# A graph network kernel on one core: the sums over the edges of one destination tile moved from TensorE to GpSimd's adding indirect transfers

## Chip, cores and metric

The kernel runs on one core of a Trainium2 chip. The metric is the device time of one execution in microseconds, as a median of runs. The profile is one execution, recorded by the hardware profiler.

## The reference, cut to what matters

There are 3125 nodes with 128 features and 53125 edges, sorted by destination (25000 random edges in both directions, and one loop per node). `x` is normalised by row and rectified, and goes through a recurrent graph network of twelve steps; then its result, added to `x`, goes through two graph convolutions.

```python
h = tanh(relu(layernorm(x)) @ W_in + b_in)
deg = clip(segment_sum(ones, dst), 1)[:, None]
for _ in range(12):
    agg = segment_sum(h[src], dst) / deg              # sums over edges: the subject here
    diff = tanh(gelu(agg @ W1 + b1) @ W2 + b2)        # 128 -> 256 -> 128
    h = h + 0.5 * (diff - relu(clearance) * h)
x = x + h
x = x + gcn(relu(gcn(relu(layernorm(x)))))            # two more sums over edges
```

## The kernel before

**Layout.** The nodes are 25 tiles of 128 (the last of 53). The seven destination groups are six of 512 nodes (the sixth, tiles 21 to 24, has 437) and group 6, `TAIL`, which is tile 20 alone: 128 nodes. `state` [128, 25, 128] f32 holds the nodes' rows. The adjacency counts `adj` stay in SBUF in f16. A sum over edges is a product with `adj`: for each of 25 source tiles, `hi` and `lo` (the two f16 halves of the scaled state) are the stationary operands and the group's columns of `adj` move past. That is 49 matmuls for a group (the short tile has both halves in one), in `edge_sums`, line 715.

**Entry.** Edges are packed into one integer each and stored in DRAM; GpSimd fetches 128 consecutive ones per window of five destinations with five indirect transfers (line 524). In 52 batches VectorE writes one-hot matrices (line 1168, two instructions for a batch), TensorE multiplies them (line 611) and ScalarE writes the counts into `adj` (line 913). Beside the first 34 batches the entry rows are computed: GpSimd normalises tile after tile (line 530, 25 instructions), TensorE transposes and multiplies them (lines 587 to 605), ScalarE applies tanh. VectorE's loop has extra work at some batches: at batch 6 the degree norms and a flag (lines 1188 to 1191), at batch 8 the first `lo` (line 1151). If the flag says that an edge was missed, a general path runs; with the reference's inputs it doesn't.

**A step** (`step`, TensorE) has this order, written out by hand: the rest of group 0's sums, group 1's sums, then for g = 2 to 6: sums of g, `outputs(g-2)` (line 757, second product, four tiles by two halves), `hidden(g-1)` (line 748, first product); after group 6, `hidden(6)`, the first eight source tiles of the next step's group 0 (`HEAD`), `outputs(5)` and `outputs(6)`. `hid` and `act_out` have one buffer for the groups 0 to 5.

The other engines follow in fixed orders too. VectorE: for g = 0 to 5, `add_bias(g-2)` (line 1295), `update(g-2)` (line 1300), `means(g)` (line 1288, sums times inverse degree); then `means(6)` and the `lo` of the next step (line 1151) between the last biases and updates. ScalarE:

```python
for g in range(1, TAIL):
    if g >= 2:
        tanh(t, g - 2)        # line 955; waits for add_bias(g - 2)
    gelu(t, g - 1)            # line 946, two instructions; waits for hidden(g - 1) and for outputs(g - 2)
act.wait_ge(s_agg, (t + 1) * NG)   # all sums of the step done: hi may be overwritten
for g in range(4):
    next_hi(t, g)             # line 857
```

`outputs(g)` waits for both instructions of `gelu(g)`. Step 1 (`first_step`) has an order of its own; step 12 (`last_step` on VectorE) also adds `x`, computes the second normalisation (lines 1363 to 1394) and the first layer's `lo` between its biases and updates. In the steps GpSimd and the DMA queues have nothing to do.

## Time and profile before

| | us |
|---|---|
| median of 3 runs | 1300.9 (1300.74 to 1300.9) |
| the profiled execution: its own time / its span | 1300.27 / 1298.5 |
| TensorE (matmul) busy | 1255.0, 97% of the span |
| VectorE busy | 400.9, 31% |
| ScalarE busy | 298.3, 23% |
| GpSimd busy | 64.4, 5% |
| line 715, share of the chain that ended last | 63% |
| line 757 / line 748, the same | 10% / 9% |
| line 1168, the same | 5% |

Busy time says which engine is loaded; the chain that ended last says what the end waited for, step by step. A matmul's record lasts longer than the interval to the next one, since matmuls overlap; so intervals are read from the chain. In tables of windows the granted clock of TensorE stands as a fraction of 2.4 GHz.

### The profile page before, as it was taken

What the parts mean: (1) busy time and instruction counts of PE and PEld (TensorE: products, weight loads), DVE (VectorE), ACT (ScalarE), POOL (GpSimd) and SP (SyncE); (2) the same over time, 40 slices, a digit from 0 to 9 for tenths busy, and PEclk for the clock granted to TensorE, in tenths of its full rate; (3) what the DMA queues carried; (4) which work ended last, traced back from release to release, by engine and by line L of the source; (5) the groups of instructions that cost most, each with busy time, mean ns of one, the idle gap of its engine ahead of it and who ended that gap; (6) DMA issues with size and microseconds to landing.
All of it is one profiled execution on the core that took longest, in us unless ns stands there. A gap on an engine that the chain in (4) does not pass through costs nothing.

```text
span 1298.5 us, 17275 instructions
## 1 busy us (share of the span) xinstructions
PE 1255.0 (97%) x7194; PEld 707.0 (54%) x7194; DVE 400.9 (31%) x817; ACT 298.3 (23%) x438; POOL 64.4 (5%) x56
## 2 busy tenths in 40 slices
PE   3888999999999999999999999999999999999998
PEld 1766465564565645645656456456564564565545
DVE  7999122131131221311312213113122132382312
ACT  1898221131121211311212113112121131120100
POOL 4940000000000000000000000000000000000000
PEclk7899999999999999999999999999999999999999
DMA  3000200000000000000000000000000000220101
GB/s 100 3 1 2 63 1 1 1 1 0 0 0 0 0 0 0 0 0 0 0 0 0 0 0 0 0 0 0 0 0 0 0 1 24 66 61 1 50 17 34
DMA packets 24552, 13.77 MB, mean 11 GB/s; under 512 B 6173, under 2 KB 23609, under 8 KB 24388
## 3 DMA queue, kind: packets, MB, share of 16 engines
q1 hardware_dynamic: 22334, 11.88, 3.4%
q10 hardware_dynamic: 1782, 1.06, 0.3%
q8 instruction: 26, 0.43, 0.1%
q0 software_dynamic: 400, 0.33, 0.1%
q14 instruction: 10, 0.08, 0.0%
HBM read 9.42 MB, written 3.44 MB: 10 GB/s over the span
## 4 chain that ended last, share of the span: by engine, by line
PE 88%; DVE 8%; issue 2%; DMA 1%; ACT 0%; DVEq 0%; SPq 0%; POOL 0%; ACTq 0%; POOLq 0%
PE ps L715 63%; PE ps L757 10%; PE ps L748 9%; DVE scratch L1168 5%; PE ps L628 3%; PE ps L829 1%; DVE lo L1151 1%; DMA adj<-packed_scratch,adj 1%; PE ps L611 0%; PE ps L571 0%; DVE cols L1367 0%; DMA adj<-in_dst_dram 0%; DVE state L1394 0%; PE ps L565 0%; DVE ps L1295 0%
## 5 line engine op out<-in xcount | busy, mean ns | idle before, releaser
L715 PE MATMUL ps<-adj,hi 128*128 128x512 f16 (+2 forms) x2275 | 747.2, 352 | 1.3 <-DVE lo L1151 1.3
L715 PE MATMUL ps<-adj,lo 128*128 128x512 f16 (+2 forms) x2184 | 730.4, 351 | 0.0
L715 PEld LDWEIGHTS ps<-adj,hi 128*128 128x128 f16 x2275 | 220.8, 97 | 228.0 <-issue 14.5
L715 PEld LDWEIGHTS ps<-adj,lo 128*128 128x128 f16 x2184 | 212.4, 97 | 224.1 <-issue 18.2
L1295 DVE TENSOR_TENSOR ps<-ps,bias 128x512 f32<-128x512 f32 (+1 forms) x84 | 53.9, 641 | 532.4 <-PE ps L757 532.4
L955 ACT ACTIVATE scratch<-ps 128x512 f32<-128x512 f32 (+1 forms) x84 | 46.3, 552 | 614.7 <-DVE ps L1295 614.6
L946 ACT ACTIVATE scratch<-ps,b1c,cols 128x512 f32<-128x512 f32 (+2 forms) x168 | 111.9, 724 | 170.7 <-PE ps L748 169.9
L757 PEld LDWEIGHTS ps<-w,scratch 128*128 128x128 f32 x1200 | 144.2, 192 | 8.1
L757 PE MATMUL ps<-w,scratch 128*128 128x128 f32 x1200 | 146.1, 275 | 0.0
L748 PE MATMUL ps<-scratch,w 128*128 128x512 f32 (+2 forms) x336 | 137.8, 538 | 0.0
L1288 DVE TENSOR_TENSOR scratch<-ps,scratch 128x512 f32<-128x512 f32 (+2 forms) x84 | 51.9, 619 | 178.7 <-PE ps L748 131.3
L1168 DVE TENSOR_TENSOR scratch<-scratch 128x1536 f16<-128x1536 f16 (+1 forms) x106 | 92.2, 940 | 0.5 <-PE ps L611 0.5
L913 ACT ACTIVATE adj<-ps 128x1500 f16<-128x1500 f32 (+1 forms) x52 | 76.0, 1480 | 14.9 <-PE ps L611 14.6
L748 PEld LDWEIGHTS ps<-scratch,w 128*128 128x128 f32 x336 | 57.3, 191 | 38.9 <-issue 37.2
L1300 DVE SCALAR_TENSOR_TENSOR state<-state,cols,scratch 128x512 f32<-128x512 f32 (+1 forms) x84 | 58.3, 694 | 47.0 <-ACT scratch L955 46.7
L611 PE MATMUL ps<-scratch 128*128 128x125 f16 x625 | 55.4, 249 | 13.2 <-DVE scratch L1168 11.9
L1151 DVE SCALAR_TENSOR_TENSOR lo<-state,cols,hi 128x512 f16<-128x512 f32 (+2 forms) x91 | 59.9, 672 | 13.6 <-ACT hi L857 12.8
L611 PEld LDWEIGHTS ps<-scratch 128*128 128x128 f16 x625 | 45.8, 110 | 29.0 <-DVE scratch L1168 25.7
L628 PE MATMUL ps<-adj,hi 128*128 128x512 f16 (+2 forms) x175 | 58.8, 353 | 1.6 <-ACT adj L933 1.6
L628 PE MATMUL ps<-adj,lo 128*128 128x512 f16 (+2 forms) x168 | 56.6, 352 | 0.0
L857 ACT ACTIVATE hi<-state,cols 128x512 f16<-128x512 f32 (+1 forms) x84 | 52.1, 669 | 19.4 <-PE ps L715 17.3
L530 POOL TENSOR_SCALAR state<-state,cols 128x128 f32<-128x128 f32 x25 | 49.2, 1981 | 11.4 <-DVE cols L1139 11.4
(143 smaller groups left out, 247.7 us busy)
## 6 DMA issues: line engine op xcount, KB each, us to landing
scratch<-rdeg_scratch SPq DMA_DIRECT2D x1, 1562.5 KB, 8.8
state<-in_x_dram SPq DMA_DIRECT2D x5, 256.0 KB, 3.7
scratch<-in_x_dram SPq DMA_DIRECT2D x5, 256.0 KB, 2.7
x_scratch<-state SPq DMA_DIRECT2D x5, 256.0 KB, 2.7
scratch<-dinv_scratch SPq DMA_DIRECT2D x5, 256.0 KB, 3.9
state<-x_scratch SPq DMA_DIRECT2D x5, 256.0 KB, 3.1
out_dram<-state SPq DMA_DIRECT2D x5, 256.0 KB
adj<-adj ACTq DMA_DIRECT2D x1, 390.6 KB, 9.1
```

What stands on the lines that cost most here:

```text
L611: return nc.tensor.matmul(target[:, :, place * WIN:(place + 1) * WIN], Lb[buf][:, b, :, i_], Rb[buf][:, b, :, i_].rearrange("p (k d) -> p ...
L628: mm = nc.tensor.matmul(ps[:, FIRST_BANK[g], 0:n], values[:, k, :], adj[:, k, c0:c0 + n], start=(at == 0 and values is hi), stop=(k == SHORT))
L715: return nc.tensor.matmul(bank, values[:, k, :], adj[:, k, c0:c0 + n], start=is_first, stop=is_last)
L748: nc.tensor.matmul(ps_hid_tail[h] if g == TAIL else ps_hid[h][:, 0:n], w1[:, h * FEAT:(h + 1) * FEAT], agg[g == TAIL][:, 0:n], start=True, ...
L757: mm = nc.tensor.matmul(ps_out[g == TAIL][:, i * FEAT:(i + 1) * FEAT], hid[g == TAIL][:, h, i * P:(i + 1) * P], w2[:, h, :], start=(h == 0 ...
L857: nc.scalar.activation(tiles_of(hi, group), tiles_of(state, group), ACT.Copy, scale=factor).then_inc(s_hi, 1)
L913: nc.scalar.activation(adj[:, :, bass.ds((i * 2 + u) * BATCH * WIN, BATCH * WIN)].rearrange("p k (b c) -> p b k c", b=BANKS), ps[:, 3 * u: ...
L946: nc.scalar.activation(hid[g == TAIL][:, h, 0:n], ps_hid_tail[h] if g == TAIL else ps_hid[h][:, 0:n], ACT.Gelu, bias=b1c[:, h:h + 1], scal ...
L1151: return V.scalar_tensor_tensor(out=lo[:, k0:k1, :], in0=values[:, k0:k1, :], scalar=0.0 if factor is None else factor, in1=hi[:, k0:k1, : ...
L1168: last_ = V.tensor_tensor(buf[:, 0:b, :, 0:w], c_.broadcast_to((128, b, m, w)), k_.broadcast_to((128, b, m, w)), ALU.is_equal)
L1295: V.tensor_tensor(p_, p_, bias_of(1, nt), ALU.add).then_inc(s_bias, 1)
L1300: V.scalar_tensor_tensor(out=tiles_of(state, g), in0=tiles_of(state, g), scalar=now_keep, in1=act_out[:, 0:n_], op0=ALU.mult, op1=ALU.add) ...
```

## The change

In steps two to twelve the sums of group 6 are no longer 49 matmuls. SP stores each updated state group in a DRAM tensor `state_scratch` (3125 rows and one row of zeros). Per step GpSimd issues 32 indirect transfers (`CAP`): the c-th fetches, for each of the 128 destinations, the state row of its c-th edge (or the zero row), and adds it to what lies in one of three places (`tail_sum`), in turn; the first in a place overwrites. A transfer waits for the one before it in its place. TensorE adds the three places and transposes the sum with three f32 matmuls with the identity. The list `tail_rows` of the edges' sources is made in the entry, with a check that every one of these destinations has at most 32 edges; otherwise the general path runs. In `step`, `hidden(4)` moves ahead of `outputs(3)`.

The core of the diff:

```diff
 # SP
+            sp.wait_ge(s_b_room, 1)
+            sp.dma_start(state_dram[NODES:NODES + 1, :]..., lo[0:2, SHORT, :].bitcast(F32)).then_inc(s_zero, 16)
...
+            def store_state(t):
+                for g in range(NG):
+                    sp.wait_ge(s_upd, t * NG + g + 1)
+                    for sbuf, dram in rows(state, state_dram, g):
+                        sp.dma_start(dram, sbuf).then_inc(s_st[g], 16)
+            store_state(1)
+            with sp.Fori(2, STEPS) as t:
+                for i in range(PLACES):
+                    sp.wait_ge(s_place[i], t * (16 * PLACE_TURNS[i]) - 16 * PLACE_TURNS[i])
+                store_state(t)
 # GpSimd, after the five transfers of line 524
+            pool.wait_ge(s_start, WCOLS + 1)
+            nc.gpsimd.indirect_dma_start(tail_rows[:, :], None, packed_dram..., tail_start).then_inc(s_tedge, 16)
+            nc.gpsimd.memset(tail_block, 0.0)
+            ...                                   # wait for it, then a chain of 5 small instructions
+            def tail_degrees():
+                pool.wait_ge(s_deg1, 1)
+                nc.gpsimd.affine_select(out=tail_block[0:WQ, 0:WIN], in_=deg[...], ...).then_inc(s_tc2, 1)
+                pool.wait_ge(s_tc2, 6)
+                nc.gpsimd.affine_select(out=tail_block[0:WQ, 0:WIN], in_=tail_block[...], ...).then_inc(s_tchk, 1)
             pool.wait_ge(s_ln, 1)
             for g, (k0, nt) in enumerate(GROUPS):
+                if g == 3:
+                    tail_degrees()
                 for k in range(k0, k0 + nt):
...
+            def gather_tail(t):
+                for g in range(NG):
+                    pool.wait_ge(s_st[g], t * (16 * parts(g)))
+                for c in range(CAP):
+                    i, turn = c % PLACES, c // PLACES
+                    before = (t - 1) * PLACE_TURNS[i] + turn
+                    if before:
+                        pool.wait_ge(s_place[i], 16 * before)
+                    nc.gpsimd.indirect_dma_start(
+                        tail_sum[i], None, state_dram, bass.IndirectOffsetOnAxis(ap=tail_rows[:, c:c + 1], axis=0),
+                        compute_op=ALU.bypass if turn == 0 else ALU.add).then_inc(s_place[i], 16)
+            for t in range(1, STEPS):
+                gather_tail(t)
 # TensorE
             def degree_total():
                 pe.wait_ge(s_deg, 1)
+                nc.tensor.matmul(ps[:, 7, 64:65], ones_col[0:WQ, :].broadcast_to((WQ, P)), deg_sum[0:WQ, :], ...)
+                pe.wait_ge(s_tchk, 1)
+                nc.tensor.matmul(ps[:, 7, 96:96 + WIN + CAP], ones_col.broadcast_to((P, P)), tail_block, ...
+                                 ).then_inc(s_degsum, 1)
-                if b == 4:
+                if b == 7:
                     degree_total()
+            def tail_sums(t):
+                def place(i):
+                    pe.wait_ge(s_place[i], t * (16 * PLACE_TURNS[i]))
+                    return nc.tensor.matmul(bank, tail_sum[i], ident[:, :], start=(i == 0), stop=(i == PLACES - 1))
+                for i in range(PLACES - 1):
+                    place(i)
+                with pe.If(missed != 0):
+                    ...
+                return place(PLACES - 1)
                         pe.wait_ge(s_aggT, t * NG + g - 1 + OPEN)
-                        edge_sums(t, g, (s_hi, s_lo), t * NG).then_inc(s_agg, 1)
+                        if g == TAIL:
+                            tail_sums(t).then_inc(s_agg, 1)
+                        else:
+                            edge_sums(t, g, (s_hi, s_lo), t * NG).then_inc(s_agg, 1)
+                    if g == TAIL - 1:
+                        hidden(t, g - 1)
                     if g >= 2:
                         outputs(t, g - 2)
-                    if g >= 1:
+                    if g >= 1 and g != TAIL - 1:
                         hidden(t, g - 1)
 # ScalarE, ahead of batch 34
+            act.wait_ge(s_trow, 1)
+            act.wait_ge(s_norms_out, 32)
 # VectorE
                 if b == 6:
                     dve.wait_ge(s_sqrt, 1)
                     V.reciprocal(dinv[0:WQ, :], root[0:WQ, :]).then_inc(s_norms, 1)
+                if b == 8:
                     dve.wait_ge(s_degsum, 1)
-                    (copy of the total, flag)
+                    (five small instructions: total, sum of the check, missing, flag, missing_row)
                 if b in LO_AT:
                     split_lo(LO_AT.index(b), LO_AT.index(b) + 1, first_scale)
...
 # in update:
+                if not isinstance(t, int) or t > 0:
+                    dve.wait_ge(s_st[g], t * (16 * parts(g)))
 # in step_scales, one small instruction more:
+                V.tensor_scalar(now_tail, tail_scale[:, bass.ds(t, 1)], 1.0, None, ALU.mult)
```

Beside this, the search constants are 753 instead of 625 wide, one more product and a few small VectorE instructions find where the tile's edges begin, and scratch places move.

## Rows read from the trace of the kernel before

**Rows 1.** Table of windows: busy us and instructions of each engine, clock, DMA.

```profile
374.61:461.18 86.57, 86.57 (x473) 47.62 (x471) 18.32 (x33) 16.75 (x28) 0.00 (x0) 1.00 0.00 0
380.00:449.00 69.00, 69.00 (x342) 35.62 (x340) 8.51 (x13) 8.26 (x13) 0.00 (x0) 1.00 0.00 0
```

**Rows 2.** Chain that ended last, step 3: start, us, engine and line.

```profile
358.90 1.78 PE ps L757 x16
360.68 1.72 PE ps L748 x4
362.40 2.76 PE ps L715 x49
365.16 1.84 PE ps L757 x16
```

**Rows 3.** Timeline of ScalarE at the tail: start, us, instruction, idle before.

```profile
361.53 0.60 ACT L955 ACTIVATE scratch<-ps 128x512 f32<-128x512 f32 x1 [10.65 <-DVE ps L1295]
362.03 1.44 ACT L946 ACTIVATE scratch<-ps,b1c,cols 128x512 f32<-128x512 f32 x2
365.20 2.56 ACT L857 ACTIVATE hi<-state,cols 128x512 f16<-128x512 f32 x4 [1.73 <-PE ps L715]
```

**Rows 4.** Timeline of VectorE, the same stretch.

```profile
360.72 0.70 DVE L1295 TENSOR_TENSOR ps<-ps,bias 128x512 f32<-128x512 f32 x1 [9.79 <-PE ps L757]
...
362.16 0.75 DVE L1300 SCALAR_TENSOR_TENSOR state<-state,cols,scratch 128x512 f32<-128x512 f32 x1 [0.74 <-ACT scratch L955]
...
376.95 0.35 DVE L1300 SCALAR_TENSOR_TENSOR state<-state,cols,scratch 128x128 f32<-128x128 f32 x1 [0.42 <-ACT scratch L955]
```

**Rows 5.** Timeline of TensorE: `outputs(4)` as recorded.

```profile
365.00 2.00 PE L757 MATMUL ps<-w,scratch 128*128 128x128 f32 x16
```

**Rows 6.** Timeline of GpSimd, the last of the five indirect transfers.

```profile
19.09 1.21 POOL L524 DMA_INDIRECT adj<-packed_scratch,adj  x1 [0.30 <-issue]
```

**Rows 7.** Line 524 by itself: from issue to landing.

```profile
DMA to landing us min/median/max: 3.1/3.4/3.6
```

**Rows 8.** DMA issues, a state group stored to DRAM: median to landing.

```profile
x_scratch<-state SPq DMA_DIRECT2D x5, 256.0 KB, 2.7
```

**Rows 9.** Timeline of GpSimd in the entry, two stretches.

```profile
38.55 1.32 POOL L530 TENSOR_SCALAR state<-state,cols 128x128 f32<-128x128 f32 x3
...
47.16 2.67 POOL L530 TENSOR_SCALAR state<-state,cols 128x128 f32<-128x128 f32 x1
```

**Rows 10.** Timeline of VectorE at batch 8 and after.

```profile
49.60 0.77 DVE L1151 SCALAR_TENSOR_TENSOR lo<-state,cols,hi 128x512 f16<-128x512 f32 x1
50.30 7.13 DVE L1168 TENSOR_TENSOR scratch<-scratch 128x1536 f16<-128x1536 f16 x8
```

**Rows 11.** Timeline of TensorE: batch 7, and a start right behind ScalarE.

```profile
48.96 1.01 PE L611 MATMUL ps<-scratch 128*128 128x125 f16 x12
...
63.08 0.30 PE L587 MATMUL ps<-ident,state 128*128 128x128 f32 x1 [0.34 <-ACT state L909]
```

**Rows 12.** Timeline of ScalarE: what released that start.

```profile
62.34 0.59 ACT L909 ACTIVATE state<-ps 128x512 f32<-128x512 f32 x1
```

**Rows 13.** GpSimd in the entry: its longest idle time.

```profile
31.68 33.67 POOL L530 TENSOR_SCALAR state<-state,cols 128x128 f32<-128x128 f32 x19 [11.38 <-DVE cols L1139]
```

**Rows 14.** Chain that ended last: small VectorE instructions, each waiting for the one before.

```profile
1162.41 0.18 DVE cols L1378
...
1162.62 0.18 DVE cols L1379
```

**Rows 15.** Chain that ended last in step 12: first and last link of VectorE's part.

```profile
1139.82 0.71 DVE ps L1295
...
1167.19 0.57 DVE lo L1151
...
1167.90 4.05 PE ps L715 x18
```

**Rows 16.** Table of windows, step 12: busy us of each engine.

```profile
1139.82:1167.90 28.08, 27.74 (x178) 16.30 (x177) 25.22 (x94) 9.06 (x17) 0.00 (x0) 1.00 0.24 69
```

More of the change, by code:

```diff
@@ L90 @@
 ROW_BOUND = 12.0
+CAP = 32
+TAIL_NODE = GROUPS[TAIL][0] * P
+PLACES = 3
+PLACE_TURNS = [len(range(i, CAP, PLACES)) for i in range(PLACES)]
+TAIL_WINDOWS = (TAIL_NODE // (WQ * WIN), TAIL_NODE % (WQ * WIN))
+assert TAIL_WINDOWS[1] + P <= WQ * WIN
 def gnn_kernel(nc, x, src, dst, W_in, b_in, W1, b1, W2, b2, clearance, G1, gb1, G2, gb2, out):
@@ L147, in gnn_kernel @@
         now_unscale = col(1)
+        missing = col(1)
+        missing_row = col(1)
+        now_tail = col(1)
         next_scale = col(1)
+        tail_scale = bound
         top = col(4)
@@ L176, in gnn_kernel @@
         assert o + 512 == SCRATCH
+        tail_sum = [w_in[:, :], bias[:, 0, :], hid[1][:, 0, :]][0:PLACES]
         half = scratch[:, :].bitcast(F16)
@@ L253, in gnn_kernel @@
         row_i = place(WINDOWS, talli)
+        tail_first, tail_base, tail_found, tail_start_f = (place(1, tall) for _ in range(4))
+        tail_start = place(1, talli)
+        tail_junk = place(CHUNK, tall)
         ones16 = place(1, tall).bitcast(F16)
@@ L337, in gnn_kernel @@
         g_degl = sem("general_degrees_loaded")
-        s_xr = [sem(f"x_reloaded{g}") for g in range(NG)]
         s_x2 = sem("x2_ready")
@@ L341, in gnn_kernel @@
         s_fac = sem("x2_factors_ready")
-        s_x2o = [sem(f"x2_stored{g}") for g in range(NG)]
         s_x2i = [sem(f"x2_reloaded{g}") for g in range(NG)]
@@ L366, in gnn_kernel @@
         s_res = sem("result_stored")
+        s_zero = sem("zero_row_stored")
+        s_tedge = sem("tail_edges_loaded")
+        s_tc2 = sem("tail_rows_chain")
+        s_tchk = sem("tail_check_ready")
+        s_mrow = sem("missing_row_ready")
+        s_trow = sem("tail_rows_ready")
+        s_tab2 = sem("tail_scales_ready")
+        s_place = [sem(f"tail_rows_added{i}") for i in range(PLACES)]
+        s_st = [sem(f"state_stored{g}") for g in range(NG)]
         block = ctx.enter_context(nc.Block())
@@ L561, in _ @@
                                  ).then_inc(s_chunk, 1)
+            nc.tensor.matmul(ps[:, WCOLS, 0:CHUNK + 2], here[:, WINDOWS:], chunk_d, start=True, stop=True
+                             ).then_inc(s_chunk, 1)
             pe.wait_ge(s_ident, 2)
@@ L739, in edge_sums @@
                 return mm
+            def tail_sums(t):
+                bank = ps_agg[2][:, 0:P]
+                def place(i):
[4 more added lines that the diff above has]
+                with pe.If(missed != 0):
+                    for k in range(TILES):
+                        c0, n = SPANS[TAIL]
+                        nc.tensor.matmul(bank, hi[:, k, :], adj[:, k, c0:c0 + n], start=False, stop=False)
+                        if k != SHORT:
+                            nc.tensor.matmul(bank, lo[:, k, :], adj[:, k, c0:c0 + n], start=False, stop=False)
+                    with pe.Fori(0, TILES) as r:
+                        add_rest(t, TAIL, bank, r)
+                return place(PLACES - 1)
             pe.wait_ge(s_last[2], 1)
@@ L1267, in _ @@
                     then(V.tensor_tensor(half_, y_, y_, ALU.mult))
-                    then(V.scalar_tensor_tensor(out=half_, in0=half_, scalar=-0.5, in1=deg[0:WQ, :], op0=ALU.mult,
+                    then(V.scalar_tensor_tensor(out=half_, in0=half_, scalar=-0.5, in1=general_deg, op0=ALU.mult,
                                                 op1=ALU.mult))
@@ L1287, in means @@
                 source = ps[:, FIRST_BANK[g], :] if first else ps_agg[2 if g == TAIL else g % 2]
+                if g == TAIL and not first:
+                    V.scalar_tensor_tensor(out=agg[1], in0=source[:, 0:n_], scalar=now_tail, in1=row[:, c0:c0 + n_],
+                                           op0=ALU.mult, op1=ALU.mult).then_inc(s_aggT, 1)
+                    return
                 V.tensor_tensor(agg[g == TAIL][:, 0:n_], source[:, 0:n_],
```

138 lines of the change are left out of this document (96 added, 42 removed).

## The prediction

> **What bounds the kernel now.** I read the table of windows first: a whole step, from 374.61 to 461.18 us, lasts 86.57 us, and TensorE is busy for all of it at full clock, while VectorE works 18.32 us, ScalarE 16.75 us, GpSimd and DMA not at all [rows 1]. So within a step every microsecond that TensorE is spared could be a microsecond less, if nothing else then ends later. The chain that ended last shows what it is spared: group 6's 49 matmuls take 2.76 us, between hidden(4), 1.72 us, and outputs(4) [rows 2]. Then the timelines of ScalarE and VectorE at that place [rows 3, 4], because a hand-written order in which nothing waits may just fit. Last the entry, where other engines set the pace [rows 9 to 14], and step 12, where the chain runs through VectorE [rows 15, 16].
>
> **The sums themselves.** 11 steps lose 2.76 us of matmuls. Three f32 matmuls of 128 by 128 come in; outputs(3), 16 matmul records in 1.78 us of the chain, holds 8 such f32 products [rows 2]; 3/8 of it, with room for the identity's loads, is about 0.65 us. TensorE's own work falls by 2.76 - 0.65 = 2.1 us a step, 23.2 us in eleven. That is the most that the change can give in the steps.
>
> **What the 2.76 us covered.** After the sums of group 5 end (358.90 us) TensorE does outputs(3) to 360.68, hidden(4) to 362.40, group 6's sums to 365.16, then outputs(4) [rows 2]. outputs(4) needs both gelu(4). ScalarE issues them after tanh(3), which waits for VectorE's bias of outputs(3); also hid has one buffer, so gelu(4) can't start before outputs(3) has read it. In the trace: bias at 360.72, tanh at 361.53, gelu 362.03 to 363.47 [rows 3, 4]. So gelu(4) ends 363.47 - 360.68 = 2.79 us after outputs(3), and today this is over 1.7 us before outputs(4) comes up. hidden(4) and the sums cover it.
>
> With the change hidden(4) goes ahead of outputs(3). outputs(3) then ends at 358.90 + 1.72 + 1.78 = 362.40, gelu(4) at 362.40 + 2.79 = 365.19, and the only work left between is 0.65 us of place sums. TensorE starts about 0.15 us behind a ScalarE end: an activation ends at 62.34 + 0.59 = 62.93 and the transpose that it held back starts at 63.08 [rows 11, 12]. outputs(4) starts at 365.34, against a recorded 365.00 today [rows 5]. **A steady step gets 0.34 us longer, with a new stall of some 2.2 us on TensorE**: 365.19 + 0.15 - 362.40 - 0.65 = 2.29. Bounds: the start of TensorE could cost 0.05 to 0.3 us, so 0.2 to 0.5 us a step. Ten steps (two to eleven): **+3.4 us** (2 to 5).
>
> What follows outputs(4) stays as it was. next_hi(0) starts behind gelu(4), at 365.1 to 365.2 as today (365.20 [rows 3]), since the place sums are long done; means(5) sits behind tanh(3) and update(3) and moves 1.7 us later on VectorE, to about 365.2, and hidden(5) wants it only after outputs(4), at 367.3. The branches and waits of tail_sums are inside the stall. now_tail, one small VectorE instruction, lies in VectorE's idle time: it works 18.32 of 86.57 us.
>
> **Step 12.** Here the chain passes from TensorE to VectorE at the bias of outputs(3), 1139.82 us, and returns at 1167.90 [rows 15]; VectorE is busy for 25.22 of those 28.08 us [rows 16]. Whatever moves that bias moves the end of that chain. outputs(3) comes 1.72 us later (hidden(4) is now ahead of it): **+1.7 us**. Bounds: 1.0, if some gaps of 28.08 - 25.22 take it up, to 2.2. The sparing of 2.1 us on TensorE is worth nothing there, as VectorE's last lo is what TensorE waits for.
>
> **The transfers.** They must be done before TensorE reaches the place sums. The last state group of a step is written at 376.95 + 0.35 = 377.30 [rows 4]; its store lands at most 2.7 us later [rows 8]: GpSimd can begin at 380.0. The sums are due at 362.40 + 86.57 = 448.97. That leaves 69.0 us [rows 1]. The nearest rows for a gather are the five in the entry: issued every 1.21 + 0.30 = 1.51 us [rows 6], landed 3.1 to 3.6 us after issue [rows 7], also 128 rows of 512 bytes. Three places in turn let a round of three take the longer of 3 x 1.51 = 4.53 us and one issue to landing with a renewed start, 3.4 + 0.3 = 3.7 us. So issuing binds: 32 x 1.51 = 48.3, and 3.4 for the last landing: 51.7 us, 17.3 us of slack. No row shows an adding transfer, which must also read its destination. Bounds: nothing more than a plain one (3.4 us), or twice its landing (6.8 us), where a round of 6.8 + 0.3 = 7.1 us gives 11 x 7.1 = 78.1 us and comes 9.1 us late. The point of decision is a round of 69.0 / 11 = 6.3 us, or an issue of 2.05 us. I take the plain row with a microsecond or two on it: hidden, cost nothing. Without the cover each microsecond of lateness costs 11 us in all.
>
> One rule speaks against this. GpSimd's instructions pay for VectorE's: beside one-hot instructions one takes 2.67 us, while VectorE waits three take 1.32 us [rows 9]. The Trainium skill (SBUF — State Buffer, in "SBUF: two separate sides") says that GpSimd can't write transfer descriptors while VectorE runs an instruction that holds the port pair they share. The trace agrees in kind. If all of VectorE's 8.51 us in the window [rows 1] were added to the issuing, it would be 60.2 us, still under 69.0; so the sum is the same by either.
>
> SP's stores have the rest of a step: store_state(t) waits for the gathers of t - 1, done 380.0 - 374.6 + 51.7 = 57 us into the step, and update needs them a step later. The loads of `x` in step 12 queue behind stores long done.
>
> **The entry.** Wider constants, the sixth product and the search of the tile's first edge lie ahead of the wait for the first window transfer and under it. The list's transfer and its chain go into GpSimd's idle 11.38 us before 31.68 [rows 13]: 1.51 + 3.4 + five instructions of under half a microsecond [rows 9] are about 7.5 us. Not hidden is the check: degree_total waits, at batch 7, for two GpSimd instructions that follow the twelfth row instruction. GpSimd gets there at 47.16; the first takes 2.67 us beside the one-hots, as the instruction that stands there today [rows 9], to 49.8. VectorE, done with batch 8 at 49.60 [rows 10], stops for the total, so the second instruction runs alone, 1.32 / 3 = 0.44 us: 50.3. TensorE, there since 48.96 + 1.01 = 49.97 [rows 11], adds 0.15 us to start and 0.3 for two tiny products: 50.8. VectorE then has five small instructions at 0.21 us [rows 14]: 51.8. Its lo starts then and not at 49.60: 2.2 us later. Two small instructions leave batch 6 (-0.3), and GpSimd, freed in the pause, gets ahead and disturbs the one-hots for a shorter time (some tenths). **+1.5 us**; bounds 0.5 (batches later have slack after all) and 4 (both GpSimd instructions at 2.67 us). The wait for the list ahead of batch 34 is free: GpSimd's last row instruction serves a transposition at batch 26, eight batches earlier.
>
> **The sum**, made against the profiled execution's 1300.27 us: +1.5 (entry) + 3.4 (ten steps) + 1.7 (step 12) = +6.6, 1306.9 us. The median of the runs is 0.6 us above that execution, so I predict **1307.5 us**, +0.5%. The bounds of the terms together give 1304 to 1312.
>
> **Rivals.**
> (a) *The adding transfers are too slow*, and the step waits for the gather: TensorE stands before the place sums, GpSimd's rounds fill the step. For it: no adding transfer in the trace, 352 of them in a row. Against it: it takes 6.3 us for a round, against 3.7 in the rows. At a doubled landing time: 9.1 x 11 = +100 us, 1407 us.
> (b) *Faster: outputs(4) isn't held*, so that 2.1 us a step is gained. This decides if gelu(4) ends before 362.40 + 0.65 = 363.05, which needs ScalarE to be done 2.1 us earlier than I find. For it: TensorE alone is full in the rows. Against: the order of ScalarE and the one buffer of hid. 1300.9 + 1.5 - 23.2 = 1279 us.
> (c) *No difference that can be measured*: the entry's check costs 0.5 us or less, the step 0.1 us, and step 12's gaps take up half: 0.3 + 1 + 0.9 = +2.2, 1303 us.
> (d) *It doesn't do what it says*: a destination with more than 32 edges sends all to the general path. In the reference's inputs the most in this tile is 26, so I leave this out.
>
> **Chances.** Forecast 0.71; (a) 0.14; (b) 0.04; (c) 0.11. A measurement of this kernel can't tell less than about 0.2%, 2.6 us. Faster by more than that: 0.04 for (b). Within: 0.11 for (c) and 0.02 of the forecast's lower end, 0.13. Slower: 0.83. The range goes from 1301.5 to 1325 us: it takes in the forecast's own 1304 to 1312, (c), and the smallest latenesses of (a); (b) and most of (a) are left out, under 0.2.
>
> **What would show it.** In a step of the changed kernel: 86.57 + 0.34 = 86.9 us from step to step; three f32 matmuls and then TensorE idle some 2.2 us, released by gelu of line 946; outputs(4) as first work behind it. GpSimd: 32 transfers within 50 to 60 us and then idle. In the entry, VectorE idle near 49.6 us for about a microsecond. Step 12: the last lo 1.7 us later, counted from the end of group 5's sums. The prediction is wrong if TensorE's wait before the place sums names a transfer, if the stall is under a microsecond, or if VectorE's part of step 12 gets shorter.

## The result and the profile of the kernel after

| | us |
|---|---|
| before, median | 1300.9 (1300.74 to 1301.15) |
| after, median of 4 | 1324.03 (1320.66 to 1327.33) |
| ratio | 1.0178, 95% interval 1.0142 to 1.0213 |
| profiled execution after: its own time / its span | 1327.33 / 1325.6 |

The change made the kernel 1.8% slower. The forecast had the direction, but +6.6 us stand against +23.1 us between the medians and +27.1 us between the two profiled executions (1325.6 - 1298.5). The four times lie in two pairs, 1320.66 and 1320.85, 1327.21 and 1327.33; the profile shows one of the upper pair.

**Where the time went.** I take one mark in every step, the start of VectorE's `means(5)` (the sums of group 5 times the inverse degree), and cut both executions at it (to within 0.1 us): step 1 to 2, step 2 to 12, the rest. The table of windows, columns as in [rows 1], first of before, then of after:

```profile
192.43:276.26 83.83, 83.83 (x432) 45.22 (x431) 16.81 (x31) 15.41 (x27) 0.00 (x0) 1.00 0.00 1
276.26:1141.85 865.59, 865.59 (x4713) 476.14 (x4711) 197.23 (x379) 167.49 (x281) 0.00 (x0) 1.00 0.01 3
1141.85:1298.50 156.65, 149.84 (x875) 82.28 (x872) 56.67 (x155) 11.95 (x22) 0.00 (x0) 1.00 0.12 34
```

```profile
199.92:285.46 85.54, 84.13 (x427) 45.42 (x425) 16.93 (x32) 15.40 (x28) 47.91 (x32) 1.00 0.27 44
285.46:1168.83 883.37, 861.76 (x4280) 468.00 (x4280) 198.39 (x389) 167.68 (x282) 479.88 (x320) 0.98 0.27 44
1168.83:1325.60 156.77, 149.31 (x832) 81.08 (x832) 56.79 (x155) 11.89 (x23) 0.00 (x0) 0.99 0.12 33
```

| part | predicted | measured |
|---|---|---|
| entry and step 1, to the first mark | +1.5 | 199.92 - 192.43 = +7.5 |
| `hidden(4)` now ahead of the mark, seen once | +1.7 (there put in step 12) | 85.54 - 83.83 = +1.7 |
| ten steps, 2 to 12 | +3.4 | 883.37 - 865.59 = +17.8 |
| the rest | 0 | +0.1 |

So two terms were wrong, the entry and the ten steps. TensorE's granted clock, 1.00 over the ten steps before, is 0.98 after.

**A step after.** Two of the steps, cut at the start of `outputs(4)`, table of windows of after:

```profile
374.66:463.17 88.51, 86.35 (x428) 46.87 (x428) 18.41 (x34) 16.84 (x30) 47.79 (x32) 0.98 0.25 42
640.23:727.09 86.86, 84.69 (x428) 45.64 (x428) 18.43 (x34) 16.64 (x30) 47.80 (x32) 1.00 0.28 43
```

The second is the step that I forecast, 86.9 us against 86.57 in [rows 1]. It is the only one of its kind: of the ten steps, nine last 88.4 to 88.5 us. They hold the same 428 matmuls; the idle time is the same (88.51 - 86.35 = 2.16 and 86.86 - 84.69 = 2.17); the busy time of TensorE is 1.66 us longer, and the clock column says 0.98. Cut finer, behind the stall that ends at 463.24 us, the table of windows shows where the clock goes:

```profile
463.24:464.44 1.20, 1.20 (x10) 1.20 (x11) 0.79 (x2) 1.20 (x3) 0.00 (x0) 1.00 0.72 204
464.44:467.84 3.40, 3.40 (x11) 2.33 (x10) 1.97 (x4) 2.16 (x4) 0.00 (x0) 0.50 0.02 5
467.84:471.24 3.40, 3.40 (x18) 1.79 (x17) 2.32 (x4) 2.36 (x5) 0.00 (x0) 1.00 0.28 77
```

TensorE starts again at full clock, is then granted 1.2 GHz in the second of these stretches, and 2.4 GHz again in the third. It isn't chance which step goes free: the fall begins 0.73, 0.97, 1.20 and 1.42 us behind the restart in four steps in turn, the fifth has none, and in the next five it begins 0.11, 0.38, 0.63, 0.88 and 1.11 us behind. Experiment 9's profile has the same drift, with two steps free. What makes it drift, I have not tested.

The stall itself, in the timelines of TensorE and of ScalarE ahead of the step that keeps its clock (the answers to [rows 3, 5]; L877 is `outputs`, L868 `hidden`, L847 the place sums, L1082 tanh, L1073 gelu, L1439 the bias):

```profile
635.52 1.95 PE L877 MATMUL ps<-w,scratch 128*128 128x128 f32 x16
637.30 0.39 PE L847 MATMUL ps<-ident,w_in 128*128 128x128 f32 x2
...
637.75 0.39 PE L847 MATMUL ps<-ident,scratch 128*128 128x128 f32 x2
640.30 2.05 PE L877 MATMUL ps<-w,scratch 128*128 128x128 f32 x16 [2.17 <-ACT scratch L1073]
```

```profile
638.32 0.60 ACT L1082 ACTIVATE scratch<-ps 128x512 f32<-128x512 f32 x1 [12.37 <-DVE ps L1439]
638.81 1.44 ACT L1073 ACTIVATE scratch<-ps,b1c,cols 128x512 f32<-128x512 f32 x2
```

and the chain that ended last there, from `outputs(3)` through the last gelu to `outputs(4)`:

```profile
635.68 1.80 PE ps L877 x16
...
639.47 0.79 ACT scratch L1073
640.26 0.04 issue
640.30 2.05 PE ps L877 x16
```

TensorE is idle 2.17 us (forecast 2.29), until both gelu of group 4 are done. It is so in each of the eleven steps; the list of waits adds them up, with the number and the longest (L626 are the gathers):

```profile
POOL w_in L626 <- DMA state_scratch<-state: 413.8, 10, 135.8
...
PE ps L877 <- ACT scratch L1073: 23.8, 11, 2.2
```

No wait of TensorE names a transfer. The page's part on DMA issues (median from issue to landing last) answers to [rows 6 to 8]:

```profile
state_scratch<-state SPq DMA_DIRECT2D x55, 256.0 KB, 2.3
...
w_in<-state_scratch,tail_rows POOLq DMA_INDIRECT x121, 3.5
bias<-state_scratch,tail_rows POOLq DMA_INDIRECT x121, 3.7
```

GpSimd's timeline has the first and the last of the 32 of one step:

```profile
392.58 1.00 POOL L626 DMA_INDIRECT w_in<-state_scratch,tail_rows  x1 [31.22 <-DMA state_scratch<-state]
...
448.27 1.55 POOL L626 DMA_INDIRECT bias<-state_scratch,tail_rows  x1 [0.30 <-issue]
```

From one to the next it is (448.27 - 392.58) / 31 = 1.80 us. The medians of the landings, 3.5 and 3.7 us, look like a plain transfer's (3.4), but they mix two kinds. In this step the first three, which overwrite, take 0.95 to 1.00 us to issue and land 2.4 to 2.6 us after it; the 29 that add take 1.54 to 1.57 us to issue, whether VectorE works beside them or not, and land after 3.2 us at first and 4.2 us towards the end. Why the landing grows within a step isn't tested.

**The entry.** The timeline of VectorE at the check (L1324 to L1329 are its five small instructions, L1284 the first `lo`, L1301 the one-hots; answers to [rows 10, 14]):

```profile
51.51 0.16 DVE L1324 TENSOR_SCALAR cols<-ps 128x1 f32<-128x1 f32 x1 [1.32 <-PE ps L678]
...
52.07 0.13 DVE L1329 TENSOR_SCALAR cols<-cols 128x1 f32<-128x1 f32 x1
52.13 0.73 DVE L1284 SCALAR_TENSOR_TENSOR lo<-state,cols,hi 128x512 f16<-128x512 f32 x1
52.79 6.94 DVE L1301 TENSOR_TENSOR scratch<-scratch 128x1536 f16<-128x1536 f16 x8
```

`lo` begins at 52.13, forecast 51.8. The pause is as I had it. What I had not is on GpSimd. Its row instructions (L602), which normalise the entry's rows, by themselves, min/median/max in ns:

```profile
L602 POOL TENSOR_SCALAR state<-state,cols x25: 443/449/23577, 32.4 to 78.8; 128x128 f32<-128x128 f32 x25
```

In the kernel before (line 530) the longest of the 25 is 2.7 us. Here one lasts 23.6 us, from 52.21, 0.08 us behind the start of that `lo`. In this stretch VectorE has no gap (23.33 us busy), and behind it TensorE stands still, since group 4's rows are not there to be transposed. Windows of after, then TensorE's timeline:

```profile
52.13:75.71 23.58, 19.23 (x181) 15.49 (x179) 23.33 (x30) 21.33 (x20) 23.58 (x2) 0.93 0.08 3
75.71:79.13 3.42, 2.00 (x9) 1.39 (x10) 0.00 (x0) 0.60 (x1) 3.42 (x9) 0.50 0.00 0
```

```profile
77.12 1.12 PE L688 MATMUL ps<-ident,state 128*128 128x128 f32 x4 [4.64 <-POOL state L602]
```

The second window shows what ends it: VectorE, which waits for TensorE to free a one-hot buffer, is idle (0.00), GpSimd gets through the instructions that it had left, and TensorE works at half clock (0.50).

### The profile page after: what moved, and what is told of

Same layout as the page of the kernel before. It is cut to its first block, busy times and chain, and to the rows that moved or that the text cites. A ratio compares the mean times of both kernels' runs of the same rounds, so it can differ in the third digit from the quotient of the medians.

```text
span 1325.6 us, 17091 instructions
## 1 busy us (share of the span) xinstructions
PE 1255.5 (95%) x6725; PEld 702.8 (53%) x6725; DVE 403.9 (30%) x839; ACT 299.1 (23%) x438; POOL 593.6 (45%) x420
## 4 chain that ended last, share of the span: by engine, by line
PE 85%; DVE 6%; issue 4%; POOL 2%; ACT 1%; DMA 1%; DVEq 0%; ACTq 0%; SPq 0%; POOLq 0%
PE ps L816 60%; PE ps L877 11%; PE ps L868 10%; PE ps L729 3%; DVE scratch L1301 3%; POOL state L602 2%; PE ps L954 1%; DVE ps L1439 1%; ACT scratch L1073 1%; DMA adj<-packed_scratch,adj 1%; DVE lo L1284 0%; PE ps L712 0%; DMA adj<-in_dst_dram 0%; DVE cols L1516 0%; PE ps L663 0%
## 5 line engine op out<-in xcount | busy, mean ns | idle before, releaser
L816 PE MATMUL ps<-adj,hi 128*128 128x512 f16 (+2 forms) x2000 | 715.7, 370 | 1.2 <-DVE lo L1284 1.2
L816 PE MATMUL ps<-adj,lo 128*128 128x512 f16 (+2 forms) x1920 | 698.8, 370 | 0.0
L626 POOL DMA_INDIRECT w_in<-state_scratch,tail_rows x121 | 182.4, 1507 | 479.9 <-DMA state_scratch<-state 413.8
L816 PEld LDWEIGHTS ps<-adj,hi 128*128 128x128 f16 x2000 | 194.6, 97 | 225.2 <-issue 11.8
L816 PEld LDWEIGHTS ps<-adj,lo 128*128 128x128 f16 x1920 | 186.7, 97 | 220.4 <-issue 14.6
L1439 DVE TENSOR_TENSOR ps<-ps,bias 128x512 f32<-128x512 f32 (+1 forms) x84 | 53.9, 641 | 566.1 <-PE ps L877 566.1
L626 POOL DMA_INDIRECT bias<-state_scratch,tail_rows x121 | 181.8, 1503 | 38.4 <-issue 36.6
L1082 ACT ACTIVATE scratch<-ps 128x512 f32<-128x512 f32 (+1 forms) x84 | 46.3, 552 | 652.5 <-DVE ps L1439 652.5
L877 PE MATMUL ps<-w,scratch 128*128 128x128 f32 x1200 | 156.2, 287 | 23.8 <-ACT scratch L1073 23.8
L626 POOL DMA_INDIRECT scratch<-state_scratch,tail_rows x110 | 163.6, 1487 | 33.5 <-issue 33.5
L877 PEld LDWEIGHTS ps<-w,scratch 128*128 128x128 f32 x1200 | 152.7, 201 | 38.2 <-ACT scratch L1073 25.9
L1073 ACT ACTIVATE scratch<-ps,b1c,cols 128x512 f32<-128x512 f32 (+2 forms) x168 | 112.8, 723 | 171.5 <-PE ps L868 170.0
L868 PE MATMUL ps<-scratch,w 128*128 128x512 f32 (+2 forms) x336 | 145.2, 562 | 0.0
L1301 DVE TENSOR_TENSOR scratch<-scratch 128x1536 f16<-128x1536 f16 (+1 forms) x106 | 91.5, 934 | 6.5 <-PE ps L712 6.3
L868 PEld LDWEIGHTS ps<-scratch,w 128*128 128x128 f32 x336 | 62.5, 205 | 43.9 <-issue 41.2
L1038 ACT ACTIVATE adj<-ps 128x1500 f16<-128x1500 f32 (+1 forms) x52 | 76.4, 1480 | 17.8 <-PE ps L712 17.6
L1284 DVE SCALAR_TENSOR_TENSOR lo<-state,cols,hi 128x512 f16<-128x512 f32 (+2 forms) x91 | 59.7, 671 | 16.2 <-ACT hi L982 15.4
L729 PE MATMUL ps<-adj,hi 128*128 128x512 f16 (+2 forms) x175 | 59.3, 356 | 1.6 <-ACT adj L1060 1.6
```

The lines of the kernel that those rows point to most:

```text
L626: nc.gpsimd.indirect_dma_start(tail_sum[i], None, state_dram, bass.IndirectOffsetOnAxis(ap=tail_rows[:, c:c + 1], axis=0), compute_op=ALU. ...
L729: mm = nc.tensor.matmul(ps[:, FIRST_BANK[g], 0:n], values[:, k, :], adj[:, k, c0:c0 + n], start=(at == 0 and values is hi), stop=(k == SHORT))
L816: return nc.tensor.matmul(bank, values[:, k, :], adj[:, k, c0:c0 + n], start=is_first, stop=is_last)
L868: nc.tensor.matmul(ps_hid_tail[h] if g == TAIL else ps_hid[h][:, 0:n], w1[:, h * FEAT:(h + 1) * FEAT], agg[g == TAIL][:, 0:n], start=True, ...
L877: mm = nc.tensor.matmul(ps_out[g == TAIL][:, i * FEAT:(i + 1) * FEAT], hid[g == TAIL][:, h, i * P:(i + 1) * P], w2[:, h, :], start=(h == 0 ...
L1038: nc.scalar.activation(adj[:, :, bass.ds((i * 2 + u) * BATCH * WIN, BATCH * WIN)].rearrange("p k (b c) -> p b k c", b=BANKS), ps[:, 3 * u: ...
```

## The experiments

The theory after reading the two traces: (1) moving `hidden(4)` ahead, together with the missing 2.76 us of matmuls, makes the stall; (2) the stall brings TensorE's clock down from 2.4 to 1.2 GHz for a while, which costs 1.66 us a step more; (3) the entry costs 1.2 us by its pause and 6 us by the one instruction that was kept out. Rivals: for (2), the transfers themselves slow TensorE; for (3), the long instruction is not the pause's doing. "The kernel after" is the changed kernel, and each edit is made in it unless said otherwise.

**1. The order back** (transfers kept, `hidden(4)` behind `outputs(3)` again).

```diff
-                    if g == TAIL - 1:
-                        hidden(t, g - 1)
                     if g >= 2:
                         outputs(t, g - 2)
-                    if g >= 1 and g != TAIL - 1:
+                    if g >= 1:
                         hidden(t, g - 1)
```

> The changed kernel with outputs(3) ahead of hidden(4) again, as before the change. Theory (the order makes the stall, the stall makes the clock fall): hidden(4) covers 1.72 us of gelu(4) again, the stall of TensorE ahead of outputs(4) shrinks from 2.17 us to about 0.5 us, the granted clock stays at full in all steps, and a step takes 86.57 - 2.1 + 0.6 = about 85.1 us against 86.86 us (full clock) and 88.51 us (with the fall) in the changed kernel; step 12's lo of VectorE comes 1.7 us earlier. In all 1324 - 11 x 3.3 = about 1288 us. Rival (the stall comes from the transfers or from tail_sums' own waits and branches): the stall stays at about 2 us wherever hidden(4) stands, and the step stays at 87 to 88.5 us.

Measured: 1291.31 us (1288.28 to 1294.44), ratio 0.992 (0.9895 to 0.9944). Windows and timeline of a step:

```profile
370.54:455.68 85.14, 84.69 (x428) 45.65 (x428) 18.42 (x34) 16.64 (x30) 47.79 (x32) 1.00 0.26 44
```

```profile
370.61 0.60 PE L877 MATMUL ps<-w,scratch 128*128 128x128 f32 x3 [0.45 <-ACT scratch L1071]
```

The stall is 0.45 us, the clock full in each step, and a step takes 85.14 us, 1.43 less than before. The transfers are all there (47.79 us of GpSimd), so in the steps they neither slow TensorE nor cost anything; the loss in the steps belongs to the order. Two of the four executions are at 1288.3 and two at 1294.4, two levels as in the kernel after; the profiled one (1294.44) has a row instruction of 23.58 us.

**2. The order alone** (kernel before, with the swap of `hidden(4)` and `outputs(3)` and nothing else).

```diff
+                    if g == TAIL - 1:
+                        hidden(t, g - 1)
                     if g >= 2:
                         outputs(t, g - 2)
-                    if g >= 1:
+                    if g >= 1 and g != TAIL - 1:
                         hidden(t, g - 1)
```

> The kernel before, with nothing changed but hidden(4) ahead of outputs(3); the sums of group 6 are the 49 matmuls. Theory: gelu(4) ends 2.79 us behind outputs(3) and only the 2.76 us of group 6's sums lie between, so outputs(4) starts 0.3 us late: a step of 86.9 us, no stall above 0.4 us, clock full, step 12 longer by 1.7 us, 1300.9 + 3.4 + 1.7 = 1306 us. Rival (the order is harmless, the loss belongs to the transfers and the short sums): 1301 us and steps of 86.57 us.

Measured: 1306.17 us (1305.23 to 1307.68), ratio 1.0039 (1.0025 to 1.0053).

```profile
367.66:454.51 86.85, 86.78 (x474) 47.75 (x472) 18.32 (x33) 16.74 (x29) 0.00 (x0) 1.00 0.00 0
```

Here is the same 86.85 us that I forecast for the changed kernel, with group 6's sums still on TensorE: the chain `outputs(3)` -> bias, tanh, gelu -> `outputs(4)` sets the step whether TensorE works or waits meanwhile. It works, and its clock stays full. The place sums save nothing as long as this chain is the longer way. The profiled execution, at 1307.68 us the slowest of the five, also shows how far the entry varies by itself: up to step 1's `means(5)` this kernel is the kernel before, and yet that mark lies at 195.26 us and not at 192.43.

**3. The stall filled** (after, with nine f32 products of identity by identity ahead of `outputs(4)`; nothing reads them).

```diff
+                        if g == TAIL:
+                            for _ in range(9):
+                                nc.tensor.matmul(ps[:, 7, 384:512], ident[:, :], ident[:, :], start=True, stop=True)
                         outputs(t, g - 2)
```

> The changed kernel with nine f32 matmuls of the identity with itself (1.9 us) put between the place sums and outputs(4); their result is read by nobody. Theory: they fit into the stall of 2.17 us and lengthen nothing; TensorE is no longer idle and its clock stays at full, so that every step takes the 86.86 us that the changed kernel shows in its one step without a fall: about 10 x 1.65 us less than the changed kernel in its profiled execution, near 1308 us. Rival (the clock falls for another reason, or the step is long for another reason): steps of 88.5 us stay, 1324 us or, with the work added, more.

Measured: 1309.13 us (1307.79 to 1312.42), ratio 1.0061 (1.0044 to 1.0078).

```profile
372.30:459.16 86.86, 86.70 (x449) 47.65 (x448) 18.42 (x34) 16.64 (x30) 47.79 (x32) 1.00 0.26 43
```

Added work that nobody needs makes the kernel 15 us faster than after, though this profile too has a row instruction of 23.6 us in its entry. The same chain, the same 86.86 us in all ten steps, and the clock full. That settles (2): the 1.66 us are the clock's, and the idle time is what brings it down. With the clock kept the kernel takes what I had forecast for it, 1307.5 us, within 2 us.

**4. A part of the stall filled** (as 3, with four products in place of nine).

```diff
-                            for _ in range(9):
+                            for _ in range(4):
```

> The changed kernel with four f32 matmuls of identity by identity, whose result nothing reads, ahead of outputs(4): they fill some 0.95 of the 2.17 us. Nothing of the time to gelu(4) changes. If a shorter idle stretch of TensorE (some 1.2 us) leaves its clock at the full 2.4 GHz: 1309 us, as with nine such matmuls. If any idle stretch here brings it down to 1.2 GHz: 1324 us, as without them. In between if it falls in some steps alone.

Measured: 1308.59 us (1307.81 to 1310.2), ratio 1.0054 (1.0037 to 1.007). Timeline and windows:

```profile
369.08 2.05 PE L877 MATMUL ps<-w,scratch 128*128 128x128 f32 x16 [1.27 <-ACT scratch L1076]
```

```profile
369.01:455.87 86.86, 85.58 (x436) 46.53 (x436) 18.43 (x34) 16.64 (x30) 47.82 (x32) 1.00 0.26 43
```

With 1.27 us of idle time a step, TensorE keeps its clock in all eleven steps that have the stall; with 2.17 us it lost it in nine of the ten steps between the marks. So the length of the idle time matters, and 0.9 us of products are enough here.

**5. The check one group earlier** (GpSimd's two instructions ahead of group 2's rows).

```diff
-                if g == 3:
+                if g == 2:
                     tail_degrees()
```

> The changed kernel with the two GpSimd instructions of tail_degrees one group earlier (ahead of the rows of group 2 and not of group 3). Theory (in the entry the check makes VectorE pause, GpSimd gets ahead in the pause, and a row instruction is then locked out for 23.6 us by one-hot instructions that follow each other without a gap): VectorE no longer pauses over a microsecond at batch 8, GpSimd isn't locked out for more than 3 us, the entry ends 1 to 3 us later than before the change and not 7.5 us: 1318 to 1321 us. Rival (the entry's 7.5 us are the work of the wider search and the list, wherever the check stands): the entry stays at about 139.5 us and the time at 1324 us. Open between them: a lock-out may also arise by chance of phase at another place.

Measured: 1320.54 us (1319.36 to 1321.93), ratio 1.0156 (1.0139 to 1.0173). The entry (up to ScalarE's last counts) ended at 133.24 us, against 139.52 in the kernel after, and no row instruction lasted over 3 us. I took this for the remedy; the next runs show that it isn't.

**6. `outputs(3)` and `hidden(4)` inside the sums** (edit 1, and in `step` these two after 12 of group 5's 25 source tiles, so that the other 13 cover gelu(4)).

```diff
+                        elif g == TAIL - 1:
+                            edge_sums(t, g, (s_hi, s_lo), t * NG, (0, 12))
+                            outputs(t, g - 2)
+                            hidden(t, g - 1)
+                            edge_sums(t, g, (s_hi, s_lo), t * NG, (12, TILES)).then_inc(s_agg, 1)
+                            continue
```

> The changed kernel, with outputs(3) and hidden(4) put inside group 5's sums, after 12 of their 25 source tiles, so that what is left of these sums (13 source tiles, some 4.5 us) covers gelu(4)'s 2.79 us. Theory (the saving of 2.1 us a step is real, and only the cover for gelu(4) was lacking): no stall before outputs(4), no fall of the clock, a step of 84.5 us, 0.6 less than with the order put back (85.14); 1291.3 - 10 x 0.6 = 1285 us, or 1283 if step 12 gains as well; the entry's 7 us stay. Rival: the wait only moves, to hidden(5) for means(5), or to the first sums of the next step for its hi and lo: a step of 85.1 or more and 1291 us or more.

Measured: 1280.93 us (1280.1 to 1281.36), ratio 0.984 (0.9823 to 0.9856): faster than both kernels.

```profile
361.94:446.36 84.42, 84.42 (x430) 45.56 (x429) 18.57 (x33) 16.70 (x28) 47.79 (x32) 1.00 0.27 44
```

```profile
361.73 0.38 PE L847 MATMUL ps<-ident,w_in 128*128 128x128 f32 x2
...
362.17 0.39 PE L847 MATMUL ps<-ident,scratch 128*128 128x128 f32 x2
362.39 1.95 PE L877 MATMUL ps<-w,scratch 128*128 128x128 f32 x16
```

TensorE is busy for the whole 84.42 us, 2.15 less than before: the 2.1 us that I had worked out as the most the change can give. The rival, that the wait only moves, is out. My expectation of 1285 us had the entry's 7 us in it; the profiled execution has no long row instruction and reaches step 1's `means(5)` at 194.06 us, 1.6 later than before, and by their times the other three are like it.

**7. The same, with the check one group earlier.**

```diff
-                if g == 3:
+                if g == 2:
                     tail_degrees()
```

> The kernel before this one, with GpSimd's part of the check one group earlier (ahead of group 2's rows). Theory: the two costs are separate and add up, so 6.3 us less (139.52 - 133.24, what it gave at the entry's end in the changed kernel): 1278 us, ratio about 0.983, faster than both kernels. Rival (the entry's end is not what sets the time, the first step takes it up): 1285 us.

Measured: 1281.95 us (1280.81 to 1287.76), ratio 0.9862 (0.9835 to 0.9888). Not 6 us less than experiment 6, but the same, and one execution of the four, which is not the profiled one, is 6 us above the others. Theory (3) is hurt: by that time an earlier check doesn't prevent the long instruction, and a check left in its place (6) doesn't always bring it.

**8. The check's end two batches later** (TensorE's two products at batch 9, VectorE's five instructions at batch 10).

```diff
-                if b == 7:
+                if b == 9:
                     degree_total()
...
-                if b == 8:
+                if b == 10:
                     dve.wait_ge(s_degsum, 1)
```

> The changed kernel, with TensorE's two products for the check at batch 9 (was 7) and VectorE's five small instructions at batch 10 (was 8), so that nothing has to wait for GpSimd there. Theory (in the entry the pause of VectorE for GpSimd costs 1.2 us or so, and in some executions it is followed by a GpSimd row instruction that is kept waiting 23.6 us, which costs 6 us more; without the pause neither happens): group 4's transpositions come as before, the entry ends at 132.5 us, every execution lies near 1318.5 us and none near 1326. Rival (the 23.6 us have nothing to do with the pause): as in the changed kernel, some executions 6 us above the others.

Measured: 1322.97 us (1319.38 to 1325.62), ratio 1.016 (1.0144 to 1.0176). A miss. VectorE still pauses at the check, now for TensorE, which is behind:

```profile
56.78 0.16 DVE L1324 TENSOR_SCALAR cols<-ps 128x1 f32<-128x1 f32 x1 [1.60 <-PE ps L678]
```

So this didn't take the pause away, and says nothing on what the pause does.

**9. The kernel after once more**, with no edit.

> The changed kernel once more, unedited, beside the kernel above. Theory: its times fall into two groups, near 1320.8 and near 1327.2 us, as its first four did, by whether GpSimd was kept waiting in that execution. Rival (the two groups are chance): times spread evenly between 1320 and 1328 us.

Measured: 1322.02 us (1321.45 to 1322.99), ratio 1.0158 (1.0145 to 1.0171). All five are nearer the lower group. Its profile shows what that group is; windows (the stretch that answers to 52.13 to 75.71 above, and the three parts between the marks) and TensorE at group 4's transpositions:

```profile
53.42:77.00 23.58, 21.40 (x203) 16.75 (x202) 23.58 (x28) 21.45 (x22) 22.51 (x10) 0.95 0.08 3
...
195.80:281.35 85.55, 84.14 (x427) 45.43 (x425) 16.94 (x32) 15.42 (x28) 47.96 (x32) 1.00 0.27 44
281.35:1163.03 881.68, 860.08 (x4280) 466.86 (x4280) 198.24 (x389) 167.45 (x282) 479.26 (x320) 0.98 0.26 45
1163.03:1319.80 156.77, 149.31 (x832) 81.09 (x832) 56.76 (x155) 11.89 (x23) 0.00 (x0) 0.99 0.12 33
```

```profile
53.26 0.80 DVE L1284 SCALAR_TENSOR_TENSOR lo<-state,cols,hi 128x512 f16<-128x512 f32 x1
```

```profile
53.49 5.12 POOL L602 TENSOR_SCALAR state<-state,cols 128x128 f32<-128x128 f32 x2
```

```profile
74.50 0.63 PE L688 MATMUL ps<-ident,state 128*128 128x128 f32 x4 [0.33 <-ACT state L1034]
```

The same program, beside the same gapless VectorE, gets its row instructions done in 2.4 to 2.7 us each, and the transpositions wait 0.33 us, not 4.64. Here the first of them starts 53.49 - 53.26 = 0.23 us behind the `lo`. The entry costs 195.80 - 192.43 = 3.4 us in place of 7.5, the ten steps 16.1 (eight with the fallen clock, two without); 3.4 + 1.7 + 16.1 + 0.1 = 21.3, the difference of the spans.

**10. Both remedies**, the edits of 6 and 8 together.

> Both remedies: outputs(3) and hidden(4) inside group 5's sums, and the check's products and instructions two batches later. Theory: 1280.9 us (the first remedy alone) less 1.2 us for the pause: 1279.7 us, with no execution at 1286 or above; ratio about 0.983, faster than both kernels. Rival: the later check makes TensorE wait for the flag before the early sums of batch 10, and nothing is gained: 1281 us.

Measured: 1282.86 us (1282.04 to 1285.5), ratio 0.9854 (0.9839 to 0.9868). No better than 6. In the profiled execution (1285.5) a row instruction lasts 19.4 us, from 56.77, and TensorE's timeline shows the same wait:

```profile
76.24 1.11 PE L688 MATMUL ps<-ident,state 128*128 128x128 f32 x4 [3.28 <-POOL state L602]
```

**11. Two places in place of three.**

```diff
-PLACES = 3
+PLACES = 2
```

> The changed kernel with two places in turn in place of three: a transfer waits for the one before the last. By the changed kernel's landing (3.6 us from issue) and 0.3 us to start, a pair takes 3.9 us, 16 pairs 62 us of the 69 us there are: the transfers are done in time, TensorE has two f32 matmuls for three (0.2 us less), and nothing comes before the end of gelu(4) anyway: 1324 us, same as with three. Rival (turns are dearer, over 4.3 us a pair): the wait before the place sums names a transfer and the step grows by 16 times the excess.

Measured: 1322.8 us (1320.23 to 1324.12), ratio 1.0157 (1.0138 to 1.0176), as with three. Only in step 12 are the transfers late, in the timeline of TensorE:

```profile
1162.44 0.46 PE L847 MATMUL ps<-ident,w_in 128*128 128x128 f32 x2 [1.55 <-DMA w_in<-state_scratch,tail_rows]
1164.91 0.80 PE L847 MATMUL ps<-ident,bias 128*128 128x128 f32 x2 [2.01 <-DMA bias<-state_scratch,tail_rows]
```

**12. One place**, the price of a late gather.

```diff
-PLACES = 3
+PLACES = 1
```

> The changed kernel with one place for all 32 transfers, each waiting for the one before it. By two places (a pair in the time of one landing and a new start, some 3.9 us) one place takes 32 x 3.9 = 125 us from the last state group's store to the sums: 56 us more than the 69 us there are. Theory: the wait before the place sums names a transfer, a step takes 87 + 56 = 143 us and all 1324 + 11 x 56 = 1940 us. Rival (transfers into one place don't pay the full landing each): a step well under 143 us.

Measured: 1941.06 us (one execution).

```profile
338.23:482.78 144.55, 86.30 (x424) 47.23 (x424) 18.51 (x33) 16.75 (x28) 49.21 (x32) 0.80 0.16 26
482.78:626.11 143.33, 85.73 (x424) 46.70 (x424) 18.50 (x33) 16.75 (x28) 49.37 (x32) 0.80 0.16 26
```

```profile
PE ps L847 <- DMA w_in<-state_scratch,tail_rows: 641.8, 11, 64.3
```

This is what rival (a) would have looked like: the wait before the place sums names a transfer and takes 58 us a step. The arithmetic by rounds, 32 times a landing and a start, gave 143 us a step; these two take 144.6 and 143.3.

## Why the prediction was right and where it was not

The direction and the chain behind it were right. That 1324.03 us lies within my range of 1301.5 to 1325 is luck: its upper part stood for transfers that come late (rival a), and they didn't; my own terms with their bounds end at 1312.

- **What the change can give, 2.1 us a step:** right, 86.57 - 84.42 = 2.15, shown in experiment 6, where nothing stands in its way.
- **The stall and its chain:** right. 2.17 us (forecast 2.29) in all eleven steps, released by gelu(4); a step at full clock is 86.86 us (forecast 86.9). By the chain, gelu(4) ends 640.26 - 637.48 = 2.78 us after `outputs(3)` (forecast 2.79), the place sums take 638.13 - 637.48 = 0.65 us, as forecast, and TensorE starts 0.04 us behind gelu and not 0.15, which is what the stall is shorter by. That 0.29 us a step comes so near to 0.34 is partly luck. I had set a start worked out from the chain (365.34) against a recorded one (365.00), where the chain has 365.16 [rows 2], so 0.16 too much; the start of TensorE was 0.11 too much; and `outputs(4)` takes 2.05 us behind a stall where it takes 1.84 in a full row, 0.21 that I left out. Experiments 1 and 2 show both halves: without the swap 85.14, with the swap alone 86.85.
- **The term that failed, "a steady step gets 0.34 us longer":** 0.29 at full clock, and 1.66 on top in nine of ten steps, since the clock falls to 1.2 GHz behind the stall. 2.9 + 9 x 1.66 = 17.8, the measured +17.8 where +3.4 stood. I had priced the stall by how much later the next work begins, and left out what speed that work then has. Filling the idle time, even by 0.9 of its 2.17 us, takes all of it back (experiments 3, 4).
- **The transfers:** hidden, as forecast, and rival (a) refuted, but with less room than I said. From issue to issue it is 1.80 us, not 1.51, and the last lands at 448.27 + 4.2 = 452.5, while the place sums come up at 463.24 - 2.17 - 0.65 = 460.4: some 8 us of slack where I had 17.3, and in step 12 only 4. The term that I had wrong is the price of adding. I took the plain row, 1.21 us to issue and 3.4 to land; an adding transfer takes 1.55 and 3.2 to 4.2. The 2.7 us that I called the most for a store to land is a median [rows 8].
- **Step 12:** right in size, +1.7. The marks show it where `means(5)` first moves. Behind the stall of step 12 TensorE's clock falls as well, and the part behind the last mark is only 0.1 us longer: VectorE's part of the chain sets the time there.
- **The entry, forecast +1.5, bounds 0.5 to 4:** the pause itself was right (`lo` at 52.13, forecast 51.8). What it comes to by step 1's `means(5)` differs between executions of the same entry: +1.6 in experiment 6, +3.4 in experiment 9, +7.5 in the profile of the kernel after, and +2.8 in experiment 2, which has no check at all. So +1.5 is neither confirmed nor refuted, and +7.5 is no property of the change alone. What the sum lacked is that a GpSimd instruction can be kept out for as long as VectorE has no gap. Of the twelve profiles with the check, the four that have such an instruction reach the mark at 199.5 to 201.0 us, the eight others at 193.7 to 196.7. Of the nine executions of the kernel after, two (1327.2 and 1327.3) lie where it would put them and seven lie between 1320.7 and 1323.0.
- **What stays open:** what decides whether a row instruction is kept out. It is not at which batch VectorE waits (10 has the long instruction in its profile), and, by the time of one execution alone, not where the check's instructions are on GpSimd (7). In the four profiles that have it (after, 1, 3 and 10) the instruction starts within 0.1 us behind the start of the VectorE instruction that opens the gapless stretch; in the nearest that doesn't (6), it starts 0.15 us behind. That speaks for a chance of timing, but it is a comparison of traces, and no run forced it. A kernel without the check, or one in which GpSimd's rows are done ahead of it, was not tried.

**What to carry to other kernels.** When work is taken off the busiest engine, look at what that work covered, and give the chain that it covered something else to hide behind: here the same edit is worth +1.8% or -1.6% by where two blocks of matmuls stand. A new stall of TensorE is to be priced twice, by its length and by the speed of what follows it, and the granted clock of the windows on both sides says which it is. Where times of one kernel fall into two groups, profile one of each before building a remedy: my first one looked right on four executions.

## What the runs showed of the hardware that I had not expected

- **A stall of 2.17 us in 86.9 us of steady matmuls brings TensorE's granted clock to half** in nine of the ten steps between the marks of the kernel after, which costs 1.66 us each time; in one, with the same idle time, it didn't, and in experiment 9 in two. The fall doesn't come with the restart but 0.1 to 1.4 us behind it, a quarter of a microsecond later from step to step. A stall of 1.27 us at the same place did so in none of eleven steps, one of 0.45 us in none.
- **One GpSimd instruction of 0.44 us took 23.6 us** beside VectorE instructions that follow each other without a gap, while in other executions of the same program its like gets in every 2.4 to 2.7 us. The Trainium skill (SBUF — State Buffer, "SBUF: two separate sides") says that of the two engines, when a VectorE instruction that reads two SBUF inputs meets a GpSimd one that reads SBUF, whichever starts first holds the shared ports for its whole instruction and blocks the other. The trace agrees that the one waits for the other; but here GpSimd did not get its turn at the end of one VectorE instruction, nor of any of some thirty (x30 in the window).
- **An indirect transfer that adds costs more than one that overwrites** (from DRAM, 128 rows of 512 bytes, kernel after, the step from 392.58 us): 1.55 us to issue against 0.95 to 1.00, with 0.30 between two, and 3.2 to 4.2 us from issue to landing against 2.4 to 2.6. They don't slow TensorE: beside them it is busy 84.42 us of 84.42 in experiment 6.
